# Three edits to the unit of a blocked state-space scan: carry on ScalarE, squares on VectorE, rows split 24 to 40

## The reference, cut to what matters

```python
def step(h, inp):
    dA_t, dB_t, x_t, C_t, t = inp
    h = h * dA_t + dB_t * x_t[:, :, None]
    nrm = jnp.sqrt(jnp.sum(h * h, axis=(1, 2), keepdims=True))
    fac = jnp.minimum(20.0 / (nrm + 1e-08), 1.0)
    h = jnp.where(t % 10 == 0, h * fac, h)
    y = jnp.einsum('bdn,bn->bd', h, C_t) + D_param * x_t
    return (h, y)
```

## Time and profile before

| | |
|---|---|
| median of 3 runs | 1541.22 us (1538.78 to 1544.27) |
| profiled execution, span from first to last instruction | 1540.7 us; no other time of it is given |
| busy share of the span | PE 95%, PEld 66%, DVE 82%, ACT 73%, POOL 61% |
| chain that ended last, largest parts | `scan` L1343 on DVE 22%, `norm` L1107 on POOL 13%, `carry` L1333 on DVE 8% |
| first scan to last scan | 436.2 us to 1326.7 us after the start |
| granted TensorE clock, mean | 0.995 |

### The profile page before, as it was taken

The page is one execution under the profiler, slowest core; times in us unless marked ns, Lnnn a source line. Parts: engine busy times, 40 slices in busy tenths (PEclk is TensorE's granted clock), DMA queues, the critical chain, the costliest instruction groups (busy, mean ns, idle before and its releaser), DMA issues.

```text
span 1540.7 us, 25357 instructions
## 1 busy us (share of the span) xinstructions
PE 1463.5 (95%) x6854; PEld 1017.9 (66%) x6854; DVE 1256.0 (82%) x2526; ACT 1122.5 (73%) x2618; POOL 934.8 (61%) x956
## 2 busy tenths in 40 slices
PE   6999999999989999999999999999999998999998
PEld 5555555555456777777777777777666665677776
DVE  7775566646468999999999999999999998788885
ACT  4454455445999999999999999999999964233243
POOL 0223313321359999999999999999999997400000
PEclk9999999999999999999999999999999999999999
DMA  8225437443757666656656666565544448466420
GB/s 268 82 64 161 133 98 208 129 146 109 241 147 204 177 165 179 172 162 184 170 154 185 172 169 184 156 174 167 139 110 109 99 102 227 119 210 198 147 86 28
DMA packets 231429, 236.27 MB, mean 153 GB/s; under 512 B 45913, under 2 KB 197145, under 8 KB 231289
## 3 DMA queue, kind: packets, MB, share of 16 engines
q1 hardware_dynamic: 230344, 233.34, 53.3%
q10 hardware_dynamic: 944, 1.31, 0.2%
HBM read 136.31 MB, written 98.56 MB: 152 GB/s over the span
## 4 chain that ended last, share of the span: by engine, by line
DVE 35%; POOL 13%; PE 11%; issue 6%; DMA 2%; DVEq 1%; POOLq 1%; SPq 0%; ACT 0%; ACTq 0%
DVE h L1343 22%; POOL rc L1107 13%; DVE banks L1333 8%; PE banks L1492 3%; PE banks L1513 3%; PE banks L1523 3%; DVE qs L1327 2%; DVEq L1341 1%; PE banks L1167 1%; DMA ub<-scratch_ub 1%; DMA q_xc<-scratch_xc 1%; DVE q_ln_st L1769 1%; DVE q_g L1678 1%; POOLq L1115 1%; DVE q_x L1650 1%
## 5 line engine op out<-in xcount | busy, mean ns | idle before, releaser
L1343 DVE TENSOR_TENSOR_SCAN h<-decay,banks 128x352 f32<-128x352 f32 x820 | 710.4, 882 | 57.6 <-DVE banks L1333 2.9
L1118 POOL TENSOR_TENSOR hc<-h,bc 128x640 f32<-128x640 f32 x410 | 592.7, 1446 | 0.0
L1167 PE MATMUL banks<-hc,w_ident 128*128 128x320 f32 (+1 forms) x1664 | 525.7, 439 | 0.1
L1236 ACT ACTIVATE tb<-dtc,a 128x320 f32<-128x320 f32 (+1 forms) x832 | 417.4, 556 | 4.8 <-DVE x L610 4.8
L1167 PEld LDWEIGHTS banks<-hc,w_ident 128*128 128x128 f32 x1664 | 284.4, 191 | 70.3 <-issue 0.4
L1258 ACT ACTIVATE decay<-tb 128x640 f32<-128x640 f32 x410 | 295.1, 723 | 0.0
L1107 POOL TENSOR_TENSOR rc<-qs,w_mhalf 128x1 f32<-128x1 f32 x410 | 224.9, 549 | 111.0 <-DVE qs L1327 111.0
L1153 PE MATMUL banks<-ub 128*128 128x176 f32 x1640 | 273.0, 289 | 2.9 <-DMA ub<-scratch_ub 2.9
L1146 PEld LDWEIGHTS banks<-sc_ss,sc_ones 128*128 128x128 f32 x820 | 123.2, 189 | 158.5 <-ACT sc_sq L1247 153.1
L1153 PEld LDWEIGHTS banks<-ub 128*128 128x128 f32 x1640 | 217.1, 193 | 3.1 <-DMA ub<-scratch_ub 3.0
L1146 PE MATMUL banks<-sc_ss,sc_ones 128*128 128x1 f32 x820 | 151.6, 254 | 37.8 <-ACT sc_sq L1247 20.3
(11 more groups left out here) (133 smaller groups left out, 1764.9 us busy)
## 6 DMA issues: line engine op xcount, KB each, us to landing
ub<-scratch_ub SPq DMA_DIRECT2D x410, 107.5 KB
bc<-scratch_blk SPq DMA_DIRECT2D x205, 160.0 KB, 3.5
scratch_ub<-turned SPq DMA_DIRECT2D x64, 512.0 KB, 3.8
scratch_ub<-spread SPq DMA_DIRECT2D x64, 176.0 KB, 3.0
scratch_xc<-xc SPq DMA_DIRECT2D x8, 1024.0 KB, 4.8
scratch_sg<-sg SPq DMA_DIRECT2D x8, 1024.0 KB, 5.9
piece<-scratch_u SPq DMA_DIRECT2D x32, 256.0 KB, 3.8
q_ys<-scratch_y SPq DMA_DIRECT2D x8, 1024.0 KB, 5.7
```

The costliest lines, as they stand in the source:

```text
L1118: pool.tensor_tensor(hc[:, pl % 2, :, at * S:(at + 1) * S] .rearrange("p (c b n) e -> p c b n e", c=KE, b=B)[:, :, b], state(m)[:, :, 0:S] ...
L1167: mm = pe.matmul(banks[:, y_bank(p), 0:KE * B * wide], w.ident[:], rhs, start=(n == 0), stop=(n == N - 1))
L1236: act.activation(tanh_rows(c, r), dtc[:, c % 2, k * B:(k + 1) * B, 0:blocks_of(c) * S].rearrange("p b (k e) -> p k b e", e=S), ACT.Tanh, s ...
L1343: dve.tensor_tensor_scan(state(m).rearrange("p r e -> p (r e)")[:, half], decay[:, m % DRING, half], psI[m % B][:, half], 0.0, ALU.mult, A ...
```

## The change

Three edits in the unit:

1. `carry` goes from DVE to ACT, as an `activation` with `Copy` and `rc` as its scale, at the place in ACT's loop at which `squares` stood. It is issued one unit ahead: `carry(m + 1)` in the round of unit `m`.
2. `squares` goes from ACT to DVE, as a `tensor_tensor_reduce` with the last column of `h` as both inputs, behind the second part of the scan. Like the form on ACT it is built as two instructions, the second of which writes out the accumulator.
3. The scan's two parts are of 24 and 40 rows where they were of 32 and 32, and PE's `inputs` waits accordingly: its first matmul for the first part and its second matmul for the second.

```diff
@@ -562,8 +562,6 @@
                 scan.tanhs(act, 0, 0, 8)
                 softplus(i, 0, KE)
         scan.tanhs(act, 0, 33, 52)
-        scan.squares(act, 0)
-        scan.squares(act, 1)
         softplus(LAST, 0, KE)
         tanh_v(LAST)
         copy_bc(LAST)
@@ -840,7 +838,9 @@
     def inp(m):
         return psI[m % B].rearrange("p (r e) -> p r e", e=W)
 
+    FIRST_ROWS = 24
     HR = NCH // 2
+    split = [slice(0, FIRST_ROWS * W), slice(FIRST_ROWS * W, NCH * W)]
 
     def state(m):
         return h[:, (m // B) % 2, m % B]
@@ -1148,8 +1148,8 @@
         def inputs(m):
             pe.wait_ge(ub_in[m % URING], 16 * (m // URING + 1))
             for c in range(KE):
-                if m >= B and c % (KE // 2) == 0:
-                    pe.wait_ge(h_ready[c // (KE // 2)], m + 1)
+                if m >= B and c < 2:
+                    pe.wait_ge(h_ready[c], m + 1)
                 mm = pe.matmul(psI[m % B][:, c * N * W:(c + 1) * N * W], ub[m % URING][:, c * P:(c + 1) * P],
                                ub[m % URING][:, E:], start=True, stop=True)
             mm.then_inc(inp_ready, 1)
@@ -1238,14 +1238,15 @@
                 dtc[:, c % 2, k * B:(k + 1) * B, 0:blocks_of(c) * S].rearrange("p b (k e) -> p k b e", e=S),
                 ACT.Tanh, scale=a16[:, r:r + 1]).then_inc(tanh_done, 1)
 
-    def squares(act, m):
+    def squares(dve, m):
         b = m % B
+        last = state(m - B)[:, :, S]
         for x in range(2):
-            act.wait_ge(h_ready[x], m + 1)
+            dve.wait_ge(h_ready[x], m + 1)
         if m >= B:
-            act.wait_ge(sum_ready, m - B + 1)
-        act.activation(sq[:, b, :], state(m - B)[:, :, S], ACT.Square,
-                       accum_out=ss[:, b:b + 1]).then_inc(sq_ready, 1)
+            dve.wait_ge(sum_ready, m - B + 1)
+        dve.tensor_tensor_reduce(sq[:, b, :], last, last, 1.0, 0.0, ALU.mult, ALU.add,
+                                 ss[:, b:b + 1]).then_inc(sq_ready, 1)
 
     def scalar(act, pre, post):
         def decays(m):
@@ -1258,6 +1259,13 @@
             act.activation(
                 decay[:, m % DRING].rearrange("p (g i e) -> p g i e", g=DB, e=W)[:, :, :, 1:],
                 tanh_block(j, b), ACT.Exp, scale=DTA_HALF / SHARP).then_inc(decay_ready, 1)
+
+        def carry(m):
+            b = m % B
+            act.wait_ge(norm_ready, m + 1)
+            act.wait_ge(inp_ready, m + 1)
+            act.activation(inp(m)[:, :, 0], state(m - B)[:, :, S], ACT.Copy, scale=rc[:, b:b + 1]
+                           ).then_inc(carry_ready, 1)
 
         def copy_y(p):
             wide = quad_blocks(p) * S
@@ -1295,12 +1303,13 @@
         pieces = {piece_unit(k): k for k in range(B, PIECES)}
         for m in range(AHEAD):
             decays(m)
+        carry(0)
         for m in range(UNITS):
             c, rows, due = rows_at(m)
             if m == 1:
                 act.wait_ge(pre.r_out, 32 * TILES)
-            if m + B < UNITS:
-                squares(act, m + B)
+            if m + 1 < UNITS:
+                carry(m + 1)
             for r in rows:
                 tanhs(act, c, r, r + 1)
             for n in due:
@@ -1326,22 +1335,15 @@
             dve.wait_ge(sum_ready, m + 1)
             dve.tensor_scalar(qs[:, b:b + 1], psQ[:, b:b + 1], 3.0e38, 1.0, ALU.min, ALU.max).then_inc(q_held, 1)
 
-        def carry(m):
-            b = m % B
-            dve.wait_ge(norm_ready, m + 1)
-            dve.wait_ge(inp_ready, m + 1)
-            dve.tensor_scalar(inp(m)[:, :, 0], state(m - B)[:, :, S], rc[:, b:b + 1], None, ALU.mult
-                              ).then_inc(carry_ready, 1)
-
         def scan(m, x):
             if x == 0:
                 dve.wait_ge(decay_ready, m + 1)
                 if m >= 2 * B:
                     dve.wait_ge(hc_ready, m - 2 * B + 1)
                 dve.wait_ge(carry_ready, m + 1)
-            half = slice(x * HR * W, (x + 1) * HR * W)
-            dve.tensor_tensor_scan(state(m).rearrange("p r e -> p (r e)")[:, half], decay[:, m % DRING, half],
-                                   psI[m % B][:, half], 0.0, ALU.mult, ALU.add).then_inc(h_ready[x], 1)
+            part = split[x]
+            dve.tensor_tensor_scan(state(m).rearrange("p r e -> p (r e)")[:, part], decay[:, m % DRING, part],
+                                   psI[m % B][:, part], 0.0, ALU.mult, ALU.add).then_inc(h_ready[x], 1)
 
 
         dve.wait_ge(pre.xc_ready, 2 * TILES)
@@ -1359,16 +1361,19 @@
                     .broadcast_to([P, KE // 2, N]),
                     b0[:, b, :, 0].unsqueeze(1).broadcast_to([P, KE // 2, N]),
                     ALU.mult).then_inc(h_ready[x], 1)
+        squares(dve, 0)
+        squares(dve, 1)
         dve.wait_ge(zeroed, 1)
         pre.dt_u(dve, TILES - 1)
         clamp(0)
         clamp(1)
         for m in range(UNITS):
-            carry(m)
             scan(m, 0)
             if B <= m + 1 < UNITS:
                 clamp(m + 1)
             scan(m, 1)
+            if m + B < UNITS:
+                squares(dve, m + B)
             k = m - UNITS + 15
             if k in (0, 3, 6, 9):
                 post.skip_first(dve, k // 3)
```

More of the change, by code:

```diff
@@ L726 @@
 Scan = namedtuple("Scan", """sync gpsimd tensor scalar vector load_first load_units tanhs decay_rates decay_scale masks
-    decay_ready y_out y_copied squares load_piece turn_piece high_piece low_piece store_piece ut_lo
+    decay_ready y_out y_copied load_piece turn_piece high_piece low_piece store_piece ut_lo
     spread_b store_b copy_bt b_split""")
@@ L1378, in scan_stage @@
     return Scan(sync, gpsimd, tensor, scalar, vector, load_first, load_units, tanhs, decay_rates, decay_scale, masks,
-                decay_ready, y_out, y_copied, squares, load_piece, turn_piece, high_piece, low_piece,
+                decay_ready, y_out, y_copied, load_piece, turn_piece, high_piece, low_piece,
                 store_piece, ut_lo, spread_b, store_b, copy_bt, b_split)
```

## The result

The changed kernel takes 1844.93 us (median of 4 runs, 1843.33 to 1850.98), the kernel before 1540.78 us in the same session (4 runs, 1538.78 to 1544.27). The ratio is 1.1983, 95% interval 1.196 to 1.2006: slower by a fifth. The forecast was 1863 us, with a range of 1560 to 1955 us.

The account below looks back on a forecast made before the run. Two loops tied as the bound, DVE's own queue and the loop over POOL, at 2.14 us a unit. 1540.7 + 307 (379 middle units) + 6 (early) + 9 (last 20) = 1863 us, range 1560 to 1955.

Parts of the forecast that it names:

- The clamp: Step in each unit: the clamp starts 0.62 us after the first scan's start, where it was 0.80.
- Carry on ACT: Step on ACT: the moved carry takes 0.36 us (0.30 to 0.45), and its loop over POOL and ACT closes at 1.96.
- Start of the squares: Step on DVE: the squares wait for the second scan and start 1.86 us after the first scan's start.
- `weigh`: Step on POOL: its product of two SBUF tiles runs from 1.42 to 2.86 us after the first scan's start.
- Squares without company: Term on DVE: without collision, squares and accumulator read hold DVE for 0.21 us (0.15 to 0.41).
- T: One unit's period, from first scan to next first scan: 2.14 us before, forecast 2.95 us after the change.
- The faster rival: No collision on DVE, as the squares need no second way into SBUF: 2.07 us a unit, 1518 us; chance 0.13.
- Squares beside `weigh`: Deciding term: the squares, with two SBUF inputs, stand until POOL's product ends; 2.95 us a unit, 307 us more; chance 0.70.
- The two rows: Earlier trace rows beside POOL's `spread`: a DVE two-tile instruction took 1.31 us, a 24-element copy 0.69 instead of 0.18.
- the copy: 24-element DVE copy beside POOL's `spread`: 0.69 us instead of 0.18, ending 0.04 us after POOL.
- The mild rival: POOL's `weigh` lets go before its end: 2.30 us a unit, 1605 us; chance 0.13 together with an emptied-pipe case.
- this case: Full collision of the squares with `weigh` in every unit: likeliest 1863 us, own range 1840 to 1955; chance 0.70.

## Why the prediction was right

- **The clamp** at 0.62: 0.61. **Carry on ACT**, 0.36 (0.30 to 0.45): 0.378 us. **Start of the squares** at 1.86: 1.85. **`weigh`** from 1.42 to 2.86: from 1.40 to 2.85. Each came from a row of before, moved by one known step.
- **Squares without company** were to hold VectorE for 0.21 us: 0.20 in the run with a PSUM input, though they are recorded with 0.27 and 0.08. T of 2.07 without collision: 2.10. The faster rival (1518 us) was rightly priced: the changed kernel takes 1523.67 us with one input in PSUM and 1519.28 us with one read.
- **Squares beside `weigh`** stand till its end. The two rows were enough to see it. The forecast took its size from the copy, which ended 0.04 us behind POOL's product. That this was near the 0.06 of the next scan was in part luck: the copy reads one tensor, the sum with one input did not stand at all, and the closer relative of the squares is the product of two SBUF tiles beside it. The mild rival, that POOL lets go before its end, is what happens for a POOL instruction with one input; `weigh` has two.
- **The size** is 1% off, and the time lies near the lower end of the range that the forecast gave this case (1840 to 1955 us). I let the next scan start 0.09 us after `weigh`; it starts 0.06 after it, near the lower end I had given, and with 0.01 to 0.02 in the earlier steps T is 2.91 for 2.95. Counted by the same units in both traces, the 378 that lay in the middle stretch take 286 us more, for 307; the 12 ahead of them 9 more, for 6, about half of it in the stretch of low clock; the 20 behind them 11 more, for 9. For these last I had read 2.75 us a unit off the length of the stretch; by their starts they took 2.49, and now 3.03. That makes 306 us for 322 in this execution; the median of the four is 6 us lower still.
- **What I said would show it** showed: POOL idle 0.95 us before `norm` for 0.17, `weigh` unchanged, ACT and PE with gaps. The granted clock is 1.00 from 479.5 to 1276 us, so PE's gaps cost no clock there.
- **What I did not see** is how near the sum comes to the loop. The forecast had it done before the clamp, and it is, but at 1001.84, only 0.10 us ahead of the clamp it feeds. At 24 rows this changes nothing; at 16 it took three quarters of what I expected.

## What to carry to other kernels

Before a small instruction is moved to VectorE, ask from where it reads and which GpSimd instruction runs at that moment: 64 elements cost 0.27 us with one input from PSUM and 1.12 us with two from SBUF beside a product of 1.45 us. Where it cannot be avoided, shorten the GpSimd instruction that holds it up: the same work in two GpSimd instructions took T from 2.91 to 2.29, though not below the 2.15 of before. And when one edit of several does the harm, run the others without it: of what was run, the split alone was the only gain.

## What the runs showed of the hardware that I had not expected

A GpSimd instruction over 640 elements with one tensor input and a constant takes 1850 ns, the product of two tensors of that size 1442 ns. Beside the first, VectorE's squares stand only for its first part and end 0.83 to 0.90 us after its start; beside the second they end 0.12 to 0.13 us behind its end, and the next scan starts before that, 0.06 us behind it. Two halves of POOL's product take 0.18 us more than the whole, 1.63 for 1.45; in the six units without squares beside the second half they take 1.58 to 1.60.
